# A fourth decay buffer for the unit behind each Gelu burst, and the shared bias as two low-rank rows

## The reference, cut to what matters

```python
# part 1: selective scan, x is (1, 4096, 512)
dt = softplus(xp_low @ W_dt + b_dt)
h  = exp(dt[..., None] * A) * h + (dt * x)[..., None] * B[:, None, :]   # per token, 512 x 16 states
y  = einsum('bdn,bn->bd', h, C) + x * D_skip
x  = x + layernorm(y)
# part 2: experts (top 2 of 8, with capacity) and the shared expert
sh = gelu(xt @ sw1 + sb1) @ sw2 + sb2
sh = sh + gelu(xt @ swd) @ swu
out = out + 0.2 * sh
x  = x + layernorm(out)
```

## Time and profile before

| | profiled execution |
|---|---|
| span, first to last instruction | 3388.4 us (median of the runs: 1.4 us more) |
| PE busy | 3100.0 us, 91% |
| DVE busy | 1812.1 us, 53% |
| ACT busy | 1633.6 us, 48% |
| POOL busy | 1384.2 us, 41% |
| chain that ended last | PE 53%, nearly all in `experts` (L2030 26%, L2071 25%) |
| stage `mix` | about 150 to 1,380 us |
| DVE scan, L790 | 473 recorded of 512, mean 1282 ns |
| DVE product, L797 | 473 recorded, mean 688 ns |

### The profile page before, as it was taken

One profiled execution on the slowest core, in us unless ns is written; L12 is line 12 of the kernel. 1 busy time (PEld: TensorE's weight loads), 2 busy tenths in 40 slices (PEclk: granted clock), 3 DMA queues, 4 the chain that ended last, 5 costly groups with the idle time before them and its releaser, 6 DMA issues.

```text
span 3388.4 us, 42962 instructions
## 1 busy us (share of the span) xinstructions
PE 3100.0 (91%) x15139; PEld 2538.6 (75%) x15139; DVE 1812.1 (53%) x2476; ACT 1633.6 (48%) x2978; POOL 1384.2 (41%) x1367
## 2 busy tenths in 40 slices
PE   6464799988989899999999999999999999999997
PEld 3243677777767777788888888888888888888886
DVE  7797989988998984441331332322313313313345
ACT  7654676666767665452332432433423424324343
POOL 2297787988988785311110121021111111211224
PEclk9655899999999999999999999999999999999999
DMA  7968678696977865930320420412312303204355
GB/s 265 303 189 250 163 229 217 203 268 183 257 192 225 230 190 186 288 95 19 88 69 13 106 60 16 119 37 54 97 20 75 78 16 100 63 10 115 75 184 161
DMA packets 273447, 466.30 MB, mean 138 GB/s; under 512 B 30817, under 2 KB 102193, under 8 KB 273234
## 3 DMA queue, kind: packets, MB, share of 16 engines
q1 hardware_dynamic: 200400, 264.91, 26.5%
q0 software_dynamic: 66720, 189.87, 21.3%
q10 hardware_dynamic: 6114, 8.79, 0.7%
HBM read 366.33 MB, written 97.16 MB: 137 GB/s over the span
## 4 chain that ended last, share of the span: by engine, by line
PE 53%; DMA 2%; DVE 2%; issue 1%; ACT 1%; POOL 0%; SPq 0%; POOLq 0%; DVEq 0%; ACTq 0%
PE c_psH L2030 26%; PE c_psY L2071 25%; PE c_psT L2021 1%; DMA out<-d_y 1%; PE c_psY L2067 0%; DVE yst L1734 0%; DMA raw<-in_w 0%; DMA W2l<-ws_d 0%; DVE hl L1754 0%; ACT h L1487 0%; DVE hl L1759 0%; DVE wgt L1923 0%; PE c_psT L2130 0%; DVE hh L1753 0%; DMA d_x1p<-x_d 0%
## 5 line engine op out<-in xcount | busy, mean ns | idle before, releaser
L1759 DVE TENSOR_TENSOR hl<-h,hh 128x512 fp32r<-128x512 f32 (+1 forms) x400 | 242.5, 606 | 1185.3 <-ACT hh L1491 1185.2
L1489 ACT ACTIVATE h<-c_psH,biases 128x512 f32<-128x512 f32 (+1 forms) x400 | 248.1, 620 | 1045.0 <-PE c_psH L2030 1033.0
L897 POOL TENSOR_TENSOR u<-dtxs,Bt 128x512 f32<-128x512 f32 x512 | 669.3, 1348 | 148.2 <-DVE b_psA L790 132.9
L790 DVE TENSOR_TENSOR_SCAN b_psA<-b_psA,b_few,u 128x512 f32<-128x512 f32 x473 | 606.4, 1282 | 75.0 <-ACT b_psA L646 74.0
L2071 PE MATMUL c_psY<-W2h,hh 128*128 128x512 f32 x1344 | 535.2, 398 | 1.8 <-DVE hl L1759 1.1
L1014 PE MATMUL b_psY<-ident,pr 128*128 128x128 f32 x2048 | 345.7, 308 | 208.2 <-DVE pr L797 190.1
L2071 PE MATMUL c_psY<-W2l,hh 128*128 128x512 f32 x1344 | 525.4, 391 | 0.0
L2071 PE MATMUL c_psY<-W2h,hl 128*128 128x512 f32 x1344 | 524.4, 390 | 0.0
L1567 POOL DMA_INDIRECT xrow<-xt_d,slot_lists x80 | 84.7, 1059 | 1050.3 <-PE c_psT L2021 600.2
L1014 PEld LDWEIGHTS b_psY<-ident,pr 128*128 128x128 f32 x2048 | 265.9, 156 | 290.8 <-DVE pr L797 238.7
L646 ACT ACTIVATE b_psA<-dts,wgt 128x512 f32<-128x512 f32 x473 | 327.4, 692 | 14.9 <-ACT b_few L635 0.2
(11 more groups left out here) (271 smaller groups left out, 5685.1 us busy)
## 6 DMA issues: line engine op xcount, KB each, us to landing
w<-ws_d POOLq DMA_DIRECT2D x224, 512.0 KB, 6.6
raw<-in_w SPq DMA_DIRECT2D x256, 256.0 KB, 2.8
Bt<-bc_d SPq DMA_DIRECT2D x64, 512.0 KB, 14.6
Ct<-bc_d SPq DMA_DIRECT2D x64, 512.0 KB, 19.1
xn<-in_x SPq DMA_DIRECT2D x8, 1024.0 KB, 7.9
xT_d<-xnT SPq DMA_DIRECT2D x8, 1024.0 KB, 12.5
dt_d<-a_dt SPq DMA_DIRECT2D x8, 1024.0 KB, 8.5
dtx_d<-a_dx SPq DMA_DIRECT2D x8, 1024.0 KB, 8.7
```

The costliest lines, as they stand in the source:

```text
L790: nc.vector.tensor_tensor_scan(a[:, :], a[:, :], u[g % U_RING][:, :], carry[:, k:k + 1], ALU.mult, ALU.add).then_inc(s_h, 1)
L897: nc.gpsimd.tensor_tensor(u[g % U_RING][:, :], dtx[s % 2][:, :], Bt[n // TG][:, n % TG, :], ALU.mult)\
L1489: nc.scalar.activation(h32[:, 0:n * P], psH[j % 2][:, 0:n * P], ACT.Gelu, bias=b1[:, j - 1:j])
L1759: nc.vector.tensor_tensor(hl[j % 2][a], h32[a], hh[j % 2][a].bitcast(F32), ALU.subtract)\
```

## The change

From unit 117 on, the unit third behind each Gelu burst (units 55, 3, 16 and 29 of a period of 64) is given an SBUF buffer `aside` in place of a PSUM bank, and its Exp is issued in the iteration of the burst, ahead of it. The other units go on alternating between the two banks, skipping it, so that the Exps of the two units that follow stand three iterations ahead of their unit instead of two. `keep` is done in order up to the unit that last had the buffer.

`shared_out` moves from the DVE (four at n = 119) to ACT (one each at n = 119 to 122) and becomes a plain scaling: sb2 comes in through the low-rank product, as two more rows (`hh0` rows of one, `L2` rows with the high and the low part of sb2). `b2bc`, its broadcast and its scaling go; `static_lo` gets three operations on two partitions, `hh0` a memset, SP one small load ahead of the first weights.

```diff
+L3B = L3 + 2
...
+        aside = sb("decay_aside", [P, CH])
+        g0, hh0 = sb("g0", [P, CH]), sb("b_low_h", [L3B, CH], F32R)
-        b2bc = sb("sb2bc", [P, D])
...
+        def is_aside(g):
+
+            return g >= WIDE and (g - 3) % NU in [at % NU for at in BURST_AT]
+
+        buffer_of = []
+        for g in range(UNITS):
+            if g < WIDE:
+                buffer_of.append(g % 3)
+            else:
+                buffer_of.append(3 if is_aside(g) else sum(not is_aside(i) for i in range(WIDE, g)) % 2)
...
-            if g < WIDE:
-                return (psA + psS[0:1])[g % 3]
-            return psA[(g - WIDE) % 2]
+            return (psA + psS[0:1] + [aside])[buffer_of[g]]
...
+            sp.dma_start(wu_raw[L3:L3B, :], w["sb2"].partition_broadcast(2)).then_inc(s_stat, 16)
             for i in range(4):
                 load_raw(i)
-            sp.dma_start(b2bc[:, :], w["sb2"].partition_broadcast(P)).then_inc(s_bias, 16)
...
-                s, n, old = g // NS, g % NS, g - (3 if g < WIDE + 2 else 2)
+                s, n, old = g // NS, g % NS, before(g)
...
-                if g == WIDE + 2:
-                    keep(old - 1)
+                while kept_units[0] <= old:
+                    keep(kept_units[0])
+                    kept_units[0] += 1
                 if old >= 0:
-                    keep(old)
                     act.wait_ge(s_cd, old + 1)
...
+            def shared_out(b, t):
...
+                nc.scalar.mul(yst[t][:, :], psS[t][:, :], SHARE).then_inc(s_yev, 1)
...
-                if g + 3 < WIDE + 2:
-                    decay(g + 3)
-                elif WIDE + 2 <= g + 2 < UNITS:
-                    decay(g + 2)
+                for a in range(g, min(g + 4, UNITS)):
+                    if (a - 3 if a < 3 or is_aside(a) else before(a)) == g:
+                        decay(a)
...
-                if g == NU:
-                    act.wait_ge(s_bias, 32)
-                    nc.scalar.mul(b2bc[:, :], b2bc[:, :], SHARE).then_inc(s_b02, 1)
...
+                    for t in range(BT):
+                        if due(b, OUT_AT + t) == g:
+                            shared_out(b, t)
...
-                nc.vector.scalar_tensor_tensor(yst[t][:, :], psS[t][:, :], SHARE, b2bc[:, :], ALU.mult, ALU.add)\
-                    .then_inc(s_yev, 1)
...
+                nc.vector.tensor_tensor(bias_low, wu_raw[two_rows, :], L2[two_rows, :].bitcast(F32),
+                                        ALU.subtract).then_inc(s_blow, 1)
...
+                nc.vector.tensor_scalar(bias_low, bias_low, ident[two_rows, L3 + 1:L3 + 2], None, ALU.mult)\
+                    .then_inc(s_blow, 1)
...
+                nc.vector.scalar_tensor_tensor(L2[two_rows, :], L2[two_rows, :].bitcast(F32), ident[two_rows, L3:L3 + 1],
+                                               bias_low, ALU.mult, ALU.add).then_inc(s_l2, 1)
```

More of the change, by code:

```diff
@@ L456, in mix, with before @@
         gate_raw = ys[1][:, 1, 0:DT * E].rearrange("p (a n) -> p a n", a=DT)
-        wu_raw = ys[1][0:L3, 2, :]
+        wu_raw = ys[1][0:L3B, 2, :]
+        bias_low = ys[1][L3:L3B, 3, :]
         def raw_pair(i):
             return hb[:, i % 4 * 2:i % 4 * 2 + 2, :]
+        def is_aside(g):
[6 more added lines that the diff above has]
+                buffer_of.append(3 if is_aside(g) else sum(not is_aside(i) for i in range(WIDE, g)) % 2)
         def bank(g):
-            if g < WIDE:
-                return (psA + psS[0:1])[g % 3]
-            return psA[(g - WIDE) % 2]
+            return (psA + psS[0:1] + [aside])[buffer_of[g]]
+        def before(g):
+            same = [i for i in range(g) if buffer_of[i] == buffer_of[g]]
+            return same[-1] if same else -1
         def split_rows(i, part):
@@ L617, in _ @@
                     for t in range(BT):
-                        if due(b, OUT_AT) + 1 + t == g:
+                        if due(b, OUT_AT + t) + 1 == g:
                             store_sh(b, t)
@@ L689, in hidden_out @@
                     act.wait_ge(s_wl, FC)
-                    act.wait_ge(s_bias, 32)
+                    act.wait_ge(s_bias, 16)
                 nc.scalar.activation(hb[:, n % HB_RING, :], psH[:, :], ACT.Identity,
@@ L715, in h_hi @@
                 nc.scalar.copy(hh[:, o:o + 2, :], hb[:, k:k + 2, :]).then_inc(s_hh, 1)
+            def shared_out(b, t):
+                if b < FB - 1:
+                    act.wait_ge(s_mm2, (b + 1) * J)
+                else:
+                    act.wait_ge(s_tile, t + 1)
+                after(act, s_sh[t], b * 16)
+                if t >= 2:
+                    act.wait_ge(s_T, min(b + 2, FB + 1) * BT)
+                    act.wait_ge(s_xt[t - 2], min(b + 2, FB + 1) * (BT // 2) * 16)
+                nc.scalar.mul(yst[t][:, :], psS[t][:, :], SHARE).then_inc(s_yev, 1)
             act.wait_ge(s_c0, 1)
@@ L731, in static_hi @@
             def static_hi():
-                act.wait_ge(s_stat, 5 * 16)
+                act.wait_ge(s_stat, 6 * 16)
                 nc.scalar.copy(L1h[:, :, 0:L3].rearrange("p a (g n) -> p a g n", g=3),
@@ L781, in _ @@
             nc.vector.memset(carry[:, :], 0.0).then_inc(s_c0, 1)
+            nc.vector.memset(hh0[L3:L3B, :].bitcast(F32), 1.0).then_inc(s_one, 1)
             dve.wait_ge(s_c0, 1)
@@ L829, in low_rank_lo @@
                     .then_inc(s_h0, 1)
[L831 to L840, removed]
-                nc.vector.scalar_tensor_tensor(yst[t][:, :], psS[t][:, :], SHARE, b2bc[:, :], ALU.mult, ALU.add)\
-                    .then_inc(s_yev, 1)
             def static_lo():
-                dve.wait_ge(s_stat, 5 * 16)
+                dve.wait_ge(s_stat, 6 * 16)
                 dve.wait_ge(s_lhi, 3)
@@ L864, in _ @@
                 for b in blocks(g):
-                    if due(b, OUT_AT) == g:
-                        for t in range(BT):
-                            shared_out(b, t)
                     if due(b, LOW_LO_AT) == g:
@@ L1039, in up @@
                     pe.wait_ge(s_llo, 2)
-                    pe.wait_ge(s_l2, 1)
+                    pe.wait_ge(s_l2, 2)
                     wh, wl = L1h, L1l
@@ L1059, in down @@
                     pe.wait_ge(s_h0, b + 1)
+                    pe.wait_ge(s_one, 1)
                     for t in range(BT):
-                        last = nc.tensor.matmul(psS[t][:, :], hh0[:, t * P:(t + 1) * P], L2[:, :], start=True, stop=False)
+                        last = nc.tensor.matmul(psS[t][:, :], hh0[0:L3B, t * P:(t + 1) * P], L2[0:L3B, :],
+                                                start=True, stop=False)
                 else:
@@ L2066, in down @@
                                 pe.wait_ge(s_yev, at["t0"] - (2 if at["k"] == 1 else 4) + min(t, 1 if at["k"] == 1 else 3) + 1)
-                            last = nc.tensor.matmul(psY[t][:, :], hh[0][0:L3, c], L2[:, :], start=True, stop=False)
+                            last = nc.tensor.matmul(psY[t][:, :], hh[0][0:L3, c], L2[0:L3, :], start=True, stop=False)
                             continue
```

14 lines of the change are left out of this document (8 added, 6 removed).

## The result

The changed kernel takes 3411.5 us (median of four runs, 3405.4 to 3415.6) against 3390.6 us for the kernel before beside it. The ratio is 1.0058, with a 95% interval of 1.0046 to 1.0070: slower by about 20 us. The forecast was 3381.2 us, the range 3362 to 3398. The profiled execution has a span of 3411.2 us against 3388.4.

What follows compares the result with a forecast made beforehand. All engines nearly full, VectorE's scan waiting for ACT's Exp the largest VectorE wait. Terms 8.8 + 6.0 - 1.2 - 1.8 - 3.2 = 8.6 us off the 3388.4 span, median 1.4 above it: 3381.2 us, range 3362 to 3398.

Steps and rivals of the forecast that it cites:

- Burst A: Gelu burst at unit 52, seven times: scan of unit 56 starts 1.31 us earlier, 1.25 taken each, 8.8 us gained.
- The port: Aside unit's two SBUF inputs make VectorE wait for POOL: 1.9 us at burst D, hidden under the stall at burst A.
- shared_out on ACT at no cost: Four shared_out on ACT at units 55 to 58, about 0.6 us each: cost 0, up to 0.5 a period.
- SyncE's store would not wait: SP's store needs the fourth shared_out, which was to end about 2 us before the store's turn.
- Burst B: Gelu burst at unit 64, six times: the 2.00 us stall goes, 1.0 us each, 6.0 gained, at most 9.6.
- PE's wait for w1: Behind burst B: POOL issues the w1 load up to 1.3 us earlier, 0.4 us taken for it.
- Burst C: Gelu burst at unit 77, six times: no stall to remove, POOL stands still 1.97 us, -0.3 each, -1.8 us.
- Burst D: Gelu burst at unit 90, six times: 1.30 us gained against waits for POOL, -0.2 each, -1.2 us.
- Start: Three small VectorE operations on two partitions at unit 10: 3.2 us lost, between 2.0 and 5.1.
- Rival 3: Stretch of burst C: POOL becomes the bound, hls comes late for ACT and PE; 3404.7 us, chance 0.18.
- Rival 2: PE's wait for the w1 load takes back what bursts A and B gave; 3394.8 us, chance 0.15.

Runs made afterwards that it cites:

- Run 3: The changed kernel with the four shared_out back on VectorE at unit 119, aside units kept: 3415.6 us, ratio 1.0047 to the kernel before.
- run 2: The changed kernel with no aside unit at all: 3398.9 us, ratio 1.0000 to the kernel before.
- run 10: The changed kernel, all four bursts, with the load of dtxs issued ahead of the last three Ct tables: 3374.6 us, ratio 0.9940 to the kernel before.
- runs 5 and 11: The changed kernel with aside units behind the first two bursts only: 3390.4 us, ratio 0.9980; the same with the dtxs load ahead of three Ct tables: 3368.7 us, 0.9927.
- Run 7: The changed kernel with GpSimd made to wait for VectorE's product of burst C's aside unit: 3399.3 us, ratio 1.0005 to the kernel before.
- runs 3 and 4: Run 3, and the changed kernel with the Exp of burst C's aside unit issued behind the burst: 3418.5 us, ratio 1.0058 to the kernel before.

## Why the prediction was wrong, step by step

- **Burst A: right in mechanism, the size near.** The stall moved to unit 56 and lasts 2.05 us, where about 2.6 were forecast; PE's adds gain 0.9 us at unit 60, where 1.25 were taken. The port's 0.54 us lie under the stall, as said.
- **shared_out on ACT at no cost: not contradicted.** Run 3 differs by 0.1%, run 2 from before by 0.0%, each plus or minus 0.1% or more. The claim that SyncE's store would not wait was wrong. SyncE issued the first store behind ACT's shared_out, at 1164.09, which is 1.9 us behind the end of the stall; before, it was issued at 988.98, 3.2 us ahead of that end (992.22). But run 3 says that this cost nothing.
- **Burst B: right, and more.** DVE's stall fell from 2.00 to 0.19 us:

```profile
1189.72 1.29 DVE L819 TENSOR_TENSOR_SCAN b_psA<-b_psA,b_few,u 128x512 f32<-128x512 f32 x1 [0.19 <-ACT b_psA L664]
```

  The adds gain 1.8 us from unit 60 to 76 (1.0 taken, 1.6 the bound). PE's wait for w1 fell from 9.5 to 7.1 us, 0.4 a period, as taken. That the sizes fit so well is partly luck: in the other runs with aside units at A and B the adds gain 0.2 to 2.9 us there.
- **Burst C: the step that failed.** The prediction took -0.3 us a period, with -11.8 in all as the far end, and gave as the reason that POOL would stand still for the aside unit. It saw that the wait is mutual and priced only POOL's half. At D it had priced DVE's half with 1.9 us. At C it left that half out, although POOL was busy there for 39.6 of 41 us, which it cites for the other half. The measured price is 4.1 us on the DVE and 5.9 us in PE's adds, of which 1.8 are PE's lower clock behind its idle times. The prediction had PE, "2 to 4 us behind the DVE there", hide most; even in run 10, where the DVE's excess is 1.7 us, PE's adds lose 1.1. A second error made the price of C that large. One POOL instruction in the way of each would have been 1.9 us. The scan passed two or three, because POOL was working off a queue behind the load of dtxs. The row of that load, 2.9 us in three waits, stands in the trace of before and I did not use it. It tells of a transfer with no slack left in front of a stretch that the change makes units reach earlier. That it would also land later was not to be read from it.
- **Burst D: right.** Forecast -0.2, measured 0.0 (+3.2 at unit 88, +3.2 at 96), and runs 5 and 11 agree. The price of the port is 0.5 + 0.9 = 1.4 us here, where 1.9 were forecast:

```profile
1252.31 1.78 DVE L819 TENSOR_TENSOR_SCAN decay_aside<-decay_aside,b_few,u 128x512 f32<-128x512 f32 x1
1254.13 1.57 DVE L826 TENSOR_TENSOR pr<-decay_aside,Ct 128x512 f32<-128x512 f32 x1
```

- **Start: right.** The three operations take 177.79 to 180.77, 2.98 us, and the adds are 3.0 us late at unit 10 (3.2 forecast; 1.3 to 5.7 in the other runs with these three operations):

```profile
177.79 1.64 DVE L872 TENSOR_TENSOR ys<-ys,L 2x512 f32<-2x512 f32 x1
179.47 0.48 DVE L875 TENSOR_SCALAR ys<-ys,ident 2x512 f32<-2x512 f32 x1
179.99 0.75 DVE L878 SCALAR_TENSOR_TENSOR L<-L,ident,ys 2x512 fp32r<-2x512 f32 x1
```

- **The rivals.** Rival 3 named the right place and sign, and at 3404.7 us was the nearest, but by another road, so that its number is near by luck: it let POOL lose time and hls come late for ACT and PE. In the changed kernel ACT and PE do not wait for hls. The DVE waits for POOL, and PE for the DVE. Rival 2 did not happen: the wait for w1 shrank. The sum with C at 5.9 in place of 0.3 would be 8.6 - 6 x 5.6 = -25 us, that is 3413 for the profiled execution, which took 3411.2.

The Trainium skill (SBUF — State Buffer, section "Who interferes with whom") has VectorE and GpSimd share one pair of ports under an exclusive lock. Run 7 agrees with it: with GpSimd still, the product is back at 0.69 us. The prediction drew on that rule for D and did not carry it to C. The rule alone, the later one blocked until the first has ended, does not give C's size: the scan of 5.44 us let three instructions end, and the measurement decides.

## What to carry to other kernels

An edit that puts an operand in the way of another engine has a price at every place where it is used, and the price depends on how full that engine's queue is there. Work out both halves of a mutual wait at each place, and leave the place out where nothing is to be gained. Before a change makes work arrive earlier, list the transfers that land just in time now, those with small waits in a few periods: one of them becomes the wall, and moving its issue can be worth more than the change.

## What the runs showed of the hardware

- A VectorE scan with two SBUF inputs need not get in at the next gap between GpSimd instructions: it let up to three GpSimd instructions pass, with a DMA issue of 0.58 us between them, and took 5.44 us in place of 1.28. At A and D of the changed kernel it waited only for the instruction that was running (1.36 to 1.82 us). That is no rule of the place: at D it took 3.97 us in three of twelve periods of runs 3 and 4, past two drives and an h_lo in the one below (run 3, DVE and POOL). Why it gets in after one or after three is open.

```profile
1257.93 3.97 DVE L805 TENSOR_TENSOR_SCAN decay_aside<-decay_aside,b_few,u 128x512 f32<-128x512 f32 x1
```

```profile
1257.09 2.50 POOL L919 TENSOR_TENSOR u<-dtxs,Bt 128x512 f32<-128x512 f32 x2
1259.55 1.26 POOL L928 TENSOR_TENSOR hls<-hb,hhs 128x512 fp32r<-128x512 f32 x1
```

- Holding GpSimd back for 1.6 us a period (9.5 in six waits) made the kernel 0.53% faster.
- A few us of idle time cost TensorE more than themselves: behind two gaps of 1.47 and 1.21 us the granted clock was 0.66 over the 5 us from 1226, where the kernel before had 1.00, and from the adds of unit 81 to those of unit 82 it took 4.99 us in place of 3.18 (means of six periods).
- With the DMA engines full (share 1.05 from 1190 to 1214), the order of issue in one queue moved the landing of a 256 KB load by 15.5 us (43.6 in place of 59.1 us behind the adds of unit 52, means of six periods in run 10 and in the changed kernel), and the whole kernel by 1.2%. Of the 15.5 us, 6.0 are its earlier issue (28.8 in place of 34.9) and 9.5 its shorter way from issue to landing (14.7 in place of 24.3).
